# A graph layer's mixture stage: features loaded first, products in pieces, the next mixture bank added earlier

## The reference, cut to what matters

```python
xn = _layernorm(x)                                   # x: 1250 x 1024
x = x + gnn(xn, edges) + mix(xn)
# gnn: h = xn @ W.T + b; out[row] = sum over edges of dis[row] * dis[col] * h[col]
# mix: q = feature_map(xn @ Wq.T + bq); kv = k_prime.T @ v per head
#      attn = q @ kv;  out = attn @ Wo.T + bo
x = x + ffn(_layernorm(x))                           # 8 experts, weighted by a router
```

## Time and profile before

| | us |
|---|---|
| median of 3 runs | 1213.19 |
| lowest, highest | 1212.43, 1213.55 |
| the profiled execution | 1213.78 |
| its span | 1211.8 |
| PE busy | 1133.4 (94%) |
| PE waiting for a feature transfer (L1661) | 21.3 |
| PE waiting for DVE at the mixture (L1661, xt) | 15.8 |
| PE waiting for ScalarE's `ln2_out` (L1697) | 8.5 |
| PE waiting for `xnL` in the first layernorm (L1467) | 7.7 |

### The profile page before, as it was taken

The page is one execution under the profiler, slowest core; times in us unless marked ns, Lnnn a source line. Parts: engine busy times, 40 slices in busy tenths (PEclk is TensorE's granted clock), DMA queues, the critical chain, the costliest instruction groups (busy, mean ns, idle before and its releaser), DMA issues.

```text
span 1211.8 us, 15068 instructions
## 1 busy us (share of the span) xinstructions
PE 1133.4 (94%) x5547; PEld 979.1 (81%) x5547; DVE 384.5 (32%) x1007; ACT 250.0 (21%) x388; POOL 293.6 (24%) x236
## 2 busy tenths in 40 slices
PE   3999999999999989999889986888799999999998
PEld 3886888878899988888668875667599999998887
DVE  5865255655531011322202112333532112111111
ACT  4431111112233343211101111322312211112000
POOL 5001201122132254300134423233303332216000
PEclk9999999999999999999989998999899999999999
DMA  5222001212243565512387766665103212114321
GB/s 190 96 69 96 12 18 54 68 57 70 64 129 108 196 241 197 168 41 98 89 263 221 221 178 187 196 181 165 53 2 113 70 56 64 57 56 166 121 96 70
DMA packets 143364, 139.28 MB, mean 115 GB/s; under 512 B 6507, under 2 KB 120507, under 8 KB 142012
## 3 DMA queue, kind: packets, MB, share of 16 engines
q1 hardware_dynamic: 141996, 135.51, 35.7%
q10 hardware_dynamic: 1296, 2.79, 0.6%
HBM read 102.32 MB, written 35.96 MB: 114 GB/s over the span
## 4 chain that ended last, share of the span: by engine, by line
PE 84%; DMA 6%; DVE 4%; ACT 3%; issue 2%; SPq 2%; DVEq 0%; ACTq 0%
PE ps L1481 9%; PE ps L1483 9%; PE ps L1482 9%; PE ps L1745 6%; PE ps L1747 6%; PE ps L1746 6%; DMA qs0L<-qT_d 3%; PE ps L1791 3%; PE ps L1792 3%; PE ps L1793 3%; PE ps L1661 3%; PE ps L1687 3%; PE ps L1682 3%; PE ps L1663 3%; PE ps L1662 3%; PE ps L1491 2%
## 5 line engine op out<-in xcount | busy, mean ns | idle before, releaser
L1481 PE MATMUL ps<-w_hi,xnH 128*128 128x512 f32 x480 | 192.2, 400 | 0.0
L1483 PE MATMUL ps<-w_hi,xnL 128*128 128x512 f32 x480 | 188.4, 392 | 0.0
L1482 PE MATMUL ps<-w_lo,xnH 128*128 128x512 f32 x480 | 188.2, 392 | 0.0
L1483 PEld LDWEIGHTS ps<-w_hi,xnL 128*128 128x128 f32 x480 | 90.7, 189 | 19.4
L1481 PEld LDWEIGHTS ps<-w_hi,xnH 128*128 128x128 f32 x480 | 91.2, 190 | 17.9
L1482 PEld LDWEIGHTS ps<-w_lo,xnH 128*128 128x128 f32 x480 | 91.2, 190 | 17.8
L751 POOL TENSOR_TENSOR cL<-cR,cH 128x1280 fp32r<-128x1280 f32 x20 | 58.7, 2937 | 145.5 <-ACT cH L967 132.8
L701 POOL TENSOR_TENSOR acc<-acc,cw 128x320 f32<-128x320 f32 x40 | 35.4, 884 | 172.9 <-ACT cw L873 172.1
L1604 PE MATMUL ps<-xnH,w_hi 128*128 128x416 f32 (+1 forms) x192 | 70.2, 366 | 3.4 <-DVE mL L1264 3.3
L1745 PE MATMUL ps<-x2H,guH 128*128 128x416 f32 (+1 forms) x192 | 69.4, 362 | 0.4 <-ACT wT L1046 0.4
L1747 PE MATMUL ps<-x2H,guL 128*128 128x416 f32 (+1 forms) x192 | 69.0, 359 | 0.0
(11 more groups left out here) (310 smaller groups left out, 2083.4 us busy)
## 6 DMA issues: line engine op xcount, KB each, us to landing
cR<-c_d SPq DMA_DIRECT2D x20, 640.0 KB, 4.4
foldin<-in SPq DMA_DIRECT2D x32, 256.0 KB, 2.7
guR<-in SPq DMA_DIRECT2D x16, 512.0 KB, 5.2
c_d<-cw SPq DMA_DIRECT2D x40, 160.0 KB
w_raw<-in SPq DMA_DIRECT2D x12, 512.0 KB, 6.7
xb<-in SPq DMA_DIRECT2D x10, 512.0 KB, 5.0
qs0H<-qT_d SPq DMA_DIRECT2D x10, 512.0 KB, 6.2
qs0L<-qT_d SPq DMA_DIRECT2D x10, 512.0 KB, 7.4
```

The lines of the kernel that those rows point to most:

```text
L1481: pe.matmul(target, xnH[:, kc, cols], wH[w][:, kc, :], start=(kc == 0), stop=False)
L1482: pe.matmul(target, xnH[:, kc, cols], wL[w][:, kc, :], start=False, stop=False)
L1483: mm = pe.matmul(target, xnL[:, kc, cols], wH[w][:, kc, :], start=False, stop=(kc == KC - 1))
```

## The change

SyncE's iteration is written anew: features first, then the store of the step before, then the counts of the next step (`load_c(i + 1)`, behind the store), the next rows, and a quarter of the products of half 1 in each of iterations 1 to 4. `load_full` is split into `load_rest` (the columns of x, for the first three tiles loaded while half 0 still runs) and `load_sum`, with semaphores of their own. On DVE, `mix` is split, and the next step's mixture bank is added ahead of this step's sums and splits. `refine` becomes `refine_row`, three `tensor_scalar` with pointers in place of four instructions. In the last step the normalized tile goes to a buffer of its own, `xz`, ScalarE's order changes (square root first, `gu_high` apart), and PE's last wait for the sums stands ahead of the last transposes. GpSimd's order stays: count_low(i+1), then add_bias(i+1).

```diff
@@ -196,6 +196,7 @@
         cH = [at(f"cH{k}", [P, NT, P], F32R, coff[k] + 5120) for k in range(4)]
+        xz = at("xz", [P, D], F32, OS + 8192)
         xt = [at(f"xt{k}", [P, D], F32, OS + (0, 4096, 16384)[k]) for k in range(3)]
@@ -357,8 +360,8 @@
         EDGE_STEPS = EDGE_PAIR + 4
-        LN_STEPS = 10
-        X2_STEPS = 9
+        LN_STEPS = 9
+        X2_STEPS = 8
         ROUTE_STEPS = 47
@@ -495,11 +498,10 @@
-            def load_m(h):
-                for half in range(2):
-                    cols = slice(4 * half, 4 * half + 4)
-                    sp.dma_start(wH[h][:, cols, :].bitcast(F32), m_d[h, 0, :, cols, :]).then_inc(in_m[h], 16)
-                    sp.dma_start(wL[h][:, cols, :].bitcast(F32), m_d[h, 1, :, cols, :]).then_inc(in_m[h], 16)
+            def load_m(h, piece):
+                cols = slice(2 * piece, 2 * piece + 2)
+                sp.dma_start(wH[h][:, cols, :].bitcast(F32), m_d[h, 0, :, cols, :]).then_inc(in_m[h], 16)
+                sp.dma_start(wL[h][:, cols, :].bitcast(F32), m_d[h, 1, :, cols, :]).then_inc(in_m[h], 16)
@@ -534,14 +537,15 @@
-            def load_full(t):
+            def load_rest(t):
                 if t >= 3:
                     sp.wait_ge(t2_done, 2 * (t - 2))
-                else:
-                    for k in range(3):
-                        sp.wait_ge(x1_st[k], 16 * (4, 3, 3)[k])
-                sp.dma_start(xt[t % 3][:, 0:W], x1_d[t][:, 0:W]).then_inc(in_xh[t % 3], 16)
-                sp.dma_start(xt[t % 3][:, W:D], x[t][:, W:D]).then_inc(in_xh[t % 3], 16)
+                sp.dma_start(xt[t % 3][:, W:D], x[t][:, W:D]).then_inc(in_rest[t % 3], 16)
+
+            def load_sum(t):
+                if t < 3:
+                    sp.wait_ge(x1_st[t], 16 * (4, 3, 3)[t])
+                sp.dma_start(xt[t % 3][:, 0:W], x1_d[t][:, 0:W]).then_inc(in_sum[t % 3], 16)
@@ -557,35 +561,45 @@
             load_c(0)
+            load_q(1)
             load_half(0)
             sp.dma_start(bob[0][:], bo[:, 0:W].to_broadcast([P, W])).then_inc(in_bo, 16)
-            load_q(1)
+            load_c(1)
             load_half(1)
             load_half(2)
-            load_c(1)
-            load_m(1)
+
             for i in range(2 * NT):
-                t = i % NT
-                if i == NT - 2:
-                    sp.wait_ge(g_done, NT)
-                    sp.dma_start(bob[1][:], bo[:, W:D].to_broadcast([P, W])).then_inc(in_bo, 16)
+                t = i - NT
                 if i + 2 < 2 * NT:
                     load_q(i + 2)
-                    load_c(i + 2)
-                else:
+                if i == NT - 1:
+                    sp.dma_start(bob[1][:], bo[:, W:D].to_broadcast([P, W])).then_inc(in_bo, 16)
+                if 1 <= i <= NT:
+                    store_half(i - 1)
+                elif i > NT:
+                    store_full(t - 1)
+                if 1 <= i and i + 1 < 2 * NT:
+                    load_c(i + 1)
+                if 2 <= i < NT - 1:
+                    load_half(i + 1)
+                if 1 <= i <= 4:
+                    load_m(1, i - 1)
+                if i == 5:
+                    sp.wait_ge(h_lo, 2 * NT)
+                if 5 <= i < 8:
+                    load_rest(i - 5)
+                if i == NT:
+                    load_sum(1)
+                    load_sum(2)
+                if i == NT + 1:
+                    load_sum(0)
+                if t >= 2 and t + 1 < NT:
+                    load_rest(t + 1)
+                    load_sum(t + 1)
+                if i + 2 >= 2 * NT:
                     sp.wait_ge(g_done, 2 * NT)
                     load_gu(i + 2 - 2 * NT)
-                if i < NT:
-                    store_half(t)
-                    if t >= 1 and t + 2 < NT:
-                        load_half(t + 2)
-                else:
-                    store_full(t)
-                if i == NT - 1:
-                    for k in range(3):
-                        load_full(k)
-                if i > NT and t + 2 < NT:
-                    load_full(t + 2)
+            store_full(NT - 1)
@@ -739,7 +753,7 @@
                 if hf:
-                    pool.wait_ge(in_xh[t % 3], 16 * (4, 3, 3)[t % 3] + 32 * (t // 3 + 1))
+                    pool.wait_ge(in_rest[t % 3], 16 * (t // 3 + 1))
                     pool.tensor_tensor(xt[t % 3][:, W:D], xt[t % 3][:, W:D], bob[1][:], ALU.add).then_inc(x_in, 1)
@@ -976,9 +990,12 @@
             def ln2_out(t):
-                act.wait_ge(x1s, NT + X2_STEPS * t + 9)
-                act.wait_ge(x1_st[t % 3], 16 * ((4, 3, 3)[t % 3] + t // 3 + 1))
-                act.activation(xt[t % 3][:], xt[t % 3][:], ACT.Identity, scale=lnw[:, t % 2, 18:19],
+                target = xz if t == NT - 1 else xt[t % 3]
+                act.wait_ge(x1s, NT + X2_STEPS * (t + 1))
+                act.wait_ge(in_sum[t % 3], 16 * (t // 3 + 1))
+                if t < NT - 1:
+                    act.wait_ge(x1_st[t % 3], 16 * ((4, 3, 3)[t % 3] + t // 3 + 1))
+                act.activation(target[:], xt[t % 3][:], ACT.Identity, scale=lnw[:, t % 2, 18:19],
                                bias=lnw[:, t % 2, 19:20]).then_inc(x2n, 1)
@@ -999,15 +1016,17 @@
                     count_high(i + 1)
+                if t == NT - 1:
+                    ln2_sqrt(t)
                 if t >= 1:
...
                         x2_hi(t - 1, h)
-                if i == 2 * NT - 1:
-                    for e in range(2):
-                        gu_high(e)
+                if 0 <= t < NT - 1:
+                    ln2_sqrt(t)
                 if t >= 0:
-                    ln2_sqrt(t)
                     ln2_out(t)
+                if t == NT - 2:
+                    gu_high(0)
@@ -1022,6 +1041,7 @@
             z_evac(2)
+            gu_high(1)
@@ -1077,6 +1097,14 @@
+            def refine_row(value, y, t, out_y, step, s):
+                dve.tensor_scalar(t, y, y, value, ALU.mult, ALU.mult).then_inc(step, 1)
+                dve.wait_ge(step, s + 1)
+                dve.tensor_scalar(t, t, -0.5, 1.5, ALU.mult, ALU.add).then_inc(step, 1)
+                dve.wait_ge(step, s + 2)
+                dve.tensor_scalar(out_y, y, t, None, ALU.mult).then_inc(step, 1)
+                dve.wait_ge(step, s + 3)
+
             def ln1_stats(t):
@@ -1317,18 +1345,24 @@
-            def mix(i):
-                hf, t = i // NT, i % NT
-                target = xt[t % 3][:, W:D] if hf else xh[:, t % 3, :]
+            def mix_target(i):
+                return xt[i % NT % 3][:, W:D] if i >= NT else xh[:, i % NT % 3, :]
+
+            def add_mixture(i):
                 dve.wait_ge(x_in, i + 1)
                 dve.wait_ge(g_done, i + 1)
-                dve.tensor_tensor(target, bank(i % 2), target, ALU.add).then_inc(g_dr, 1)
+                dve.tensor_tensor(mix_target(i), bank(i % 2), mix_target(i), ALU.add).then_inc(g_dr, 1)
+
+            def add_sums(i):
                 dve.wait_ge(g_dr, i + 1)
                 dve.wait_ge(a_done, i + 1)
-                dve.scalar_tensor_tensor(out=target, in0=bank(5 + i % 2), scalar=dis[:, t:t + 1], in1=target,
-                                         op0=ALU.mult, op1=ALU.add).then_inc(a_dr, 1)
+                dve.scalar_tensor_tensor(out=mix_target(i), in0=bank(5 + i % 2), scalar=dis[:, i % NT:i % NT + 1],
+                                         in1=mix_target(i), op0=ALU.mult, op1=ALU.add).then_inc(a_dr, 1)
+
+            def sum_stats(i):
+                hf, t = i // NT, i % NT
                 dve.wait_ge(a_dr, i + 1)
-                dve.bn_stats(stats0[:, t, 6 * hf:6 * hf + 6], target).then_inc(x1s, 1)
+                dve.bn_stats(stats0[:, t, 6 * hf:6 * hf + 6], mix_target(i)).then_inc(x1s, 1)
@@ -1353,13 +1387,19 @@
+            add_mixture(0)
             for i in range(2 * NT):
                 t = i - NT
-                if t >= 1:
+                if i + 1 < 2 * NT:
+                    add_mixture(i + 1)
+                add_sums(i)
+                if 1 <= t < NT - 1:
                     x2_low(t - 1)
-                mix(i)
+                sum_stats(i)
                 if t >= 0:
                     ln2(t)
+                if t == NT - 1:
+                    x2_low(t - 1)
             x2_low(NT - 1)
@@ -1694,7 +1734,7 @@
                         kc = 4 * h + k
-                        mm = pe.transpose(bank(2 + h)[:, k * P:(k + 1) * P], xt[t % 3][:, kc * P:(kc + 1) * P], ident[:])
+                        mm = pe.transpose(bank(2 + h)[:, k * P:(k + 1) * P], (xz if t == NT - 1 else xt[t % 3])[:, kc * P:(kc + 1) * P], ident[:])
                     mm.then_inc(t2_done, 1)
@@ -1749,8 +1789,8 @@
             router(1)
+            pe.wait_ge(a_dr, 2 * NT)
             x2_transposes(NT - 1)
-            pe.wait_ge(a_dr, 2 * NT)
             expert(0, 0)
```

More of the change, by code:

```diff
@@ L268, in gps_layer @@
         in_xh = [sem(f"in_xh{k}") for k in range(3)]
+        in_rest = [sem(f"in_rest{k}") for k in range(3)]
+        in_sum = [sem(f"in_sum{k}") for k in range(3)]
```

(9 more changed lines are left out.)

## The result

The changed kernel takes 1190.99 us (median of 4 runs, 1190.39 to 1193.43) against 1213.37 for the kernel before in the same comparison: a ratio of 0.9819, 95% interval 0.9802 to 0.9836. The forecast was 1194.3, range 1182 to 1207. The profiled execution has a span of 1189.5 us.

The account below looks back on a forecast made before the run. The prediction saw PE waiting in the mixture stage and the start, then a loop of 12.47 us a turn. Gains 12.1 + 1.5 + 5.3 = 18.9 us; 1213.78 - 0.6 - 18.9 = 1194.3, range 1182 to 1207.

Parts of the forecast that it names:

- The loop: Mixture stage: add_sums, store, cR load, cH, cL, bias, add_mixture, next add_sums form one serial turn, 12.47 us; 64%, 1194 us.
- The landing of cR behind the store: Mixture stage, in each turn: from the issue of cR to the start of cH, 5.0 us, ends 4.36 and 5.7.
- The change of halves: Between half 0 and half 1: ln2_out(0) waits for load_sum(0), nothing to 4.4 us, taken as 2.2.
- A(0) and A(1): Starts of add_sums in steps 0 and 1 on DVE: forecast 615.0 and 629.5, before 618.48 and 635.69.
- my 2.0 extra: First turn of the stage: load_q(3) ahead of load_c(2) and the second start loads add 2 us to a plain turn.
- A(18) to the first expert: From add_sums of step 18 to the first expert matmul: 14.0 us, before 20.1; experts start 12.1 us earlier.
- The start: First layernorm: refine_row avoids TENSOR_TENSORs held by GpSimd; transposes(2) from 27.89 to 22.6, 5.3 us gained, ends 2 and 7.
- PE is without a wait from there to 595: Between transposes(2) and the mixture stage PE never waits, so the 5.3 us gained in the start stays.
- The clock: First expert matmuls: without the long wait they are not at the low clock, 1.5 us more gained.
- The rival of 2 us waits that lower the clock: Mixture stage: waits of 2 us per step might bring more PE stretches at 1.2 GHz, 0.6 us a step; 9%, 1204 us.
- pointers held up by GpSimd: Start and tail: pointer scalars stop like TENSOR_TENSOR; start gives 1 for 5.3, tail waits some 4 again; 13%, 1203 us.
- The open loop: Mixture stage: x_in is always early, PE sets the pace with steps of 9.97 and 11.0 us; 5%, 1157 us.

## Why the prediction was right, step by step

- **The loop** decided, and it was read from the order of the queues and from rows of before. A turn was forecast at 12.47; the mean of the 17 was 12.69 (215.65 us), with the extra for the change of halves in it. The landing of cR behind the store, my weakest term, was 5.4 for the 5.0 I took; each part on the engines was right within 0.15 in the turn shown.
- **The change of halves**: I gave the wait for load_sum(0) 2.2 us. The turn was 13.97, 1.3 over the mean, and moving that transfer took 1.6 off it.
- **A(0) and A(1)**, counted from the first mixture matmul at 587.63: 20.7 and 33.6 us; forecast 19.1 and 33.6. A(0) gained 1.9 for the 3.5 of my sum, and A(1) was right only because two terms erred against each other: the first turn was an ordinary one of 12.93, without my 2.0 extra.
- **A(18) to the first expert**: 13.9, forecast 14.0. I had put this down to ScalarE's new order and to refine_row together; the runs show that either of the two parts of the change, refine_row (14.5) or all the rest (14.4), is enough by itself.
- **The start**: transposes(2) came at 22.79, forecast 22.6. The stage began 8.3 us earlier in the profile, not 5.3. The difference is not the change's: from transposes(2) to the first mixture matmul it is 568.0 us in the profiled run of before, 564.8 in that of after, and 563.2 to 566.9 in the twelve other kernels. In the kernel with the old refine, where transposes(2) come at 28.41, it is 563.5. Why these runs differ by some us, and why that of before is the longest, I did not settle. My sentence that PE is without a wait from there to 595 was wrong, too: the kernel before has 8.7 us of short waits there (3.3 in four for `mL`, 2.9 in three for `qF`, 2.3 and 0.2). They did not eat the gain.
- **The sum by terms**, in the two profiled runs: start 8.3 for 5.3; first mixture matmul to A(18) 4.6 for 6.0, all of it ahead of A(1); A(18) to the experts 6.2 for 6.1; from there to the end 3.3 for 1.5. The total is 22.3 for 18.9: the two outer terms came out larger by 4.8 us, in part by the differences between runs told above and below, and the stage smaller by 1.4.
- **The clock**: 1.5 us for experts that do not start at the low clock; first expert to end was 3.3 us shorter, the first matmul 0.43 for 0.70. In the twelve other kernels this stretch is either 3.2 to 3.3 or 1.4 to 1.8 us shorter than before, with a first matmul of 0.43 or 0.44 in all of them, so half of the 3.3 is nothing that the change controls. The rival of 2 us waits that lower the clock did not come: 0.96 and 0.95 were granted in the stage, before 0.94 and 0.95. But the waits do go with a lower clock: it was 0.99 when they were cut.
- **refine_row by itself**: 5.6 (start), 5.6 (tail) and about 1.5 (clock) are 12.7; measured 12.4. Taken out of the changed kernel it costs 9.1, since there the rest of the change covers the tail. It is thus 9 to 12 of the 22 us of the change; I had put the tail's 6 us down with the stage.
- **Rivals**: pointers held up by GpSimd, no: the three instructions ran in 0.15 to 0.28 us. The section "Who interferes with whom" of the Trainium skill, "SBUF — State Buffer", says of `tensor_scalar` that it can contend with GpSimd, when its operands meet certain conditions. I had read it as if it always did. These 128x1 operands did not contend, which does not contradict the page. The open loop, had it been true, was priced at 1157 and gives 1147.6: I kept the slow first turn in it (14.5 us by my sum, 9.98 measured), which was the loop's as well; that is 4.5 of the 9.4.

The size of the miss on the other side is the lesson: the forecast was right, and what the trace offered beyond the 22 us of the change was twice as much again, in an order of two instructions that I had read as fixed.

## What to carry to other kernels

When an instruction is moved ahead on an in-order engine, list what it waits for, and follow each of these back: if the chain returns to an instruction that now stands behind it, the program has become a loop, and its length is the step time as soon as it is longer than the step of the busiest engine (here 12.7 us against 9.97 and 10.88). Cut it where all such loops meet (here, the addition that does not need the counts goes ahead of the subtraction that does), since a cut elsewhere can leave the next longest one (here 11.76), and test it with a dose: an instruction in the loop costs its full length each turn, outside of it nothing. A store ahead of a load in one queue puts the store's producer into that chain.

## What the runs showed of the hardware

- A DMA share of 0.79 at 226 GB/s was no limit: the same transfers went at 263 GB/s and 0.90 once the order let them, with cR landing 5.4 and 5.3 us after its issue (620 to 730 us).
- On 128x1 values in fp32, DVE's TENSOR_TENSOR took 0.16 us with GpSimd idle, and while GpSimd subtracted 128x1024 tiles it ended when the subtraction in progress did: those that start at 860.28, 862.04 and 864.53 end at 862.01, 864.30 and 866.60, and the four subtractions from 857.20, 2.35 us each, end at 861.9, 864.2 and 866.6. So it cost what was left of the subtraction, up to 2.3 us, and TENSOR_SCALAR, with an immediate or with one or two pointers, took 0.15 to 0.28 us in such stretches.
